# Four transformer layers on one core: in the first layer, another order of the two sequences' energies, the closing norm and the low output sums

## The reference

```
# layer 0, for each token: 16 heads of 16 features
q = x @ Wq;  k = mask * (ctx @ Wk);  v = ctx @ Wv         # 256 -> 256 each
e[x, y] = sum_h q[h, x] * k[h, y]                         # 16 x 16 energies per token
a = softmax_y(e)
o[x, h] = sum_y a[x, y] * v[h, y]
x = layer_norm(x + o @ Wo)                                # * g1 + b1
x = layer_norm(x + relu(x @ W1 + b1) @ W2 + b2)           # * g2 + b2: the closing norm
# layers 1 to 3: each two attentions over 128 tokens and a feed-forward part
```

## Time and profile before

| what | us |
|---|---|
| median of three runs | 2115.61 |
| lowest and highest of them | 2114.29, 2116.65 |
| the profiled execution's own time | 2115.66 |
| its span in the trace | 2113.9 |

### The profile page before, as it was taken

One profiled execution on the slowest core, in us unless ns is written; L12 is line 12 of the kernel. 1 busy time (PEld: TensorE's weight loads), 2 busy tenths in 40 slices (PEclk: granted clock), 3 DMA queues, 4 the chain that ended last, 5 costly groups with the idle time before them and its releaser, 6 DMA issues.

```text
span 2113.9 us, 34721 instructions
## 1 busy us (share of the span) xinstructions
PE 1821.7 (86%) x12417; PEld 1354.7 (64%) x12417; DVE 1280.2 (61%) x2220; ACT 1073.9 (51%) x3134; POOL 996.0 (47%) x1233
## 2 busy tenths in 40 slices
PE   5766666778988998888999999999999999999997
PEld 4655555655665665665666767767667676766766
DVE  5877777856446446446357575674764736546472
ACT  1111111157556557557556555564555656656562
POOL 4566666556346336336425443553544334323340
PEclk8898888877887888887899999999999999999999
DMA  7300000000020000000000200000000000000000
GB/s 192 114 6 5 6 5 5 6 5 1 6 85 1 6 6 1 6 6 1 6 6 7 85 1 6 7 7 6 1 11 1 6 6 2 26 6 1 11 1 11
DMA packets 31361, 35.92 MB, mean 17 GB/s; under 512 B 3196, under 2 KB 30040, under 8 KB 30808
## 3 DMA queue, kind: packets, MB, share of 16 engines
q1 hardware_dynamic: 31192, 33.70, 5.3%
HBM read 31.60 MB, written 2.10 MB: 16 GB/s over the span
## 4 chain that ended last, share of the span: by engine, by line
PE 52%; DVE 13%; ACT 9%; issue 5%; POOL 3%; DVEq 0%; POOLq 0%; ACTq 0%
PE ps L580 27%; PE ps L783 6%; PE ps L722 5%; PE ps L793 5%; PE ps L827 4%; ACT work L957 3%; ACT work L964 2%; DVE work L1151 2%; DVE xn L1011 2%; DVE rowmax L1155 2%; PE ps L593 2%; PE ps L808 1%; POOL work L1344 1%; DVE O L1185 1%; ACT hT L876 1%
## 5 line engine op out<-in xcount | busy, mean ns | idle before, releaser
L580 PE MATMUL ps<-hT,w_slot 128*128 128x256 f32 x1696 | 408.5, 394 | 23.0 <-ACT hT L876 22.0
L1268 POOL TENSOR_TENSOR work<-KT,own_head 128x512 f32<-128x512 f32 x256 | 262.8, 1048 | 285.2 <-PE ps L783 179.8
L580 PEld LDWEIGHTS ps<-hT,w_slot 128*128 128x128 f32 x1696 | 322.4, 196 | 82.6 <-ACT hT L876 27.5
L964 ACT ACTIVATE work<-work,rowmax 128x128 f32<-128x128 f32 x768 | 245.0, 392 | 168.1 <-DVE rowmax L1155 167.4
L793 PEld LDWEIGHTS ps<-ident,work 128*128 128x128 f32 x1536 | 199.3, 153 | 169.8 <-issue 89.8
L957 ACT ACTIVATE work<-ps,rowmax,score_scale 128x128 f32<-128x128 f32 x512 | 229.0, 481 | 119.8 <-DVE rowmax L1159 119.0
L793 PE MATMUL ps<-ident,work 128*128 128x128 f32 x1536 | 265.7, 301 | 17.6 <-ACT work L964 17.2
L783 PE MATMUL ps<-work,QT 128*128 128x512 f32 x512 | 266.4, 605 | 9.7 <-POOL work L1268 4.6
L1344 POOL TENSOR_SCALAR work<-work,winv 128x128 f32<-128x128 f32 x512 | 185.7, 387 | 166.4 <-DVE winv L1171 164.2
L1185 DVE RECIPROCAL O<-ps 128x128 f32<-128x128 f32 x128 | 122.2, 955 | 174.7 <-PE ps L827 174.0
L950 ACT ACTIVATE work<-ps 128x512 f32<-128x512 f32 x256 | 150.8, 596 | 91.0 <-PE ps L793 90.8
(11 more groups left out here) (128 smaller groups left out, 3417.4 us busy)
## 6 DMA issues: line engine op xcount, KB each, us to landing
ctx_in<-in_ctx SPq DMA_DIRECT2D x32, 256.0 KB, 2.7
w_slot<-in_L_xattn_W SPq DMA_DIRECT2D x2, 1024.0 KB, 6.4
w_slot<-in_L_xattn_ff_w SPq DMA_DIRECT2D x1, 2048.0 KB, 11.4
w_slot<-in_L_xattn_ffn_w SPq DMA_DIRECT2D x2, 1024.0 KB, 9.7
w_slot<-in_L_xattn_w SPq DMA_DIRECT2D x2, 1024.0 KB, 8.5
out<-x_all SPq DMA_DIRECT2D x8, 256.0 KB, 2.1
x_all<-in_x SPq DMA_DIRECT2D x1, 1536.0 KB, 11.7
pad<-in_mask_Bx1x1xS_fk SPq DMA_DIRECT2D x1, 1024.0 KB, 9.6
```

What stands on the lines that cost most here:

```text
L580: mm = pe.matmul(dst, lhsT(k), rhs(k), start=(k == 0), stop=(k == chunks - 1))
L964: ex = act.activation(prob[i % NPF][:, tok(h)], src[:, tok(h)], ACT.Exp, bias=shifts[:, at:at + 1])
L1268: pool.tensor_tensor(KB[u % NK].rearrange("p (h k) -> p h k", h=HU), keys, own_head[:, e:HC:2].unsqueeze(2).broadcast_to([P, HU, S]), ALU. ...
```

## The change

Three things are moved; no instruction's form or count changes.

1. The closing `norm`, `scale` and `post` of the ending stream are taken out of the phase and put into the next one, at slots 0, 3 and 7 (`LOCAL_LEFT_SLOT`). There they belong to the stream that is then being mixed. `join` returns them apart, and `joined_pass` hands them on as `left` and `later`. At the end of the first layer they fall into the first two phases of the second.
2. A, of the second sequence, is moved from step 1 to step 4 on VectorE and GpSimd, and its sums on TensorE from step 3 to step 6, behind `tin`. On VectorE the sum, the norms and the closing norm come between the two A.
3. L of the first sequence is moved ahead of B of the second on VectorE. GpSimd's B of the second sequence is moved behind the closing `post`.

```diff
--- before.py
+++ after.py
@@ -142,6 +142,9 @@
 PLAN = [layer_plan(layer) for layer in range(NL)]
 
 
+LOCAL_LEFT_SLOT = {"norm": 0, "scale": 3, "post": 7}
+
+
 def join(layer, after, end, start, tail):
 
 
@@ -157,8 +160,8 @@
     tin = [spot for piece, spot, _, _ in first if piece == "tin"][0]
     pieces = [(at.get(piece, y2 + spot - tin), start, piece, arg, n) for piece, spot, arg, n in first]
     after_y2 = [piece for piece, _, _, _ in last].index("y2") + 2
-    pieces += [(spot, end if i < after_y2 else tail, piece, arg, n) for i, (piece, spot, arg, n) in enumerate(last)]
-    return pieces
+    pieces += [(spot, end, piece, arg, n) for piece, spot, arg, n in last[:after_y2]]
+    return pieces, [(LOCAL_LEFT_SLOT[piece], tail, piece, arg, n) for piece, _, arg, n in last[after_y2:]]
 
 
 SHIFTED = ("norm", "tin", "bias", "post")
@@ -431,13 +434,18 @@
 
                 return ahead(layer, after, st, {"norm": max([slot for slot, _, piece, _, _ in pieces if piece == "keys"], default=9)})
 
-            def joined_pass(layer, g, after):
-
-                for m in range(len(PLAN[layer]) // 2 - 1):
-                    attend(layer, g, 1, m, chain(layer, g, 0, m + 1))
+            def joined_pass(layer, g, after, left):
+
+                last = len(PLAN[layer]) // 2 - 1
+                for m in range(last):
+                    attend(layer, g, 1, m, chain(layer, g, 0, m + 1) + left)
                     attend(layer, g, 0, m + 1, chain(layer, g, 1, m + 1))
-                attend(layer, g, 1, len(PLAN[layer]) // 2 - 1, joined(layer, g, after, 0))
-                attend(*after, 0, 0, joined(layer, g, after, 1))
+                    left = []
+                pieces, later = joined(layer, g, after, 0)
+                attend(layer, g, 1, last, pieces + left)
+                pieces, left = joined(layer, g, after, 1)
+                attend(*after, 0, 0, pieces + later)
+                return left
 
             def ahead_pass(layer, g, after, left):
 
@@ -460,12 +468,12 @@
 
             together(None, 0, chain(0, 0, 0, 0), late)
             attend(0, 0, 0, 0, chain(0, 0, 1, 0))
+            left = []
             for layer in range(FIRST_AHEAD):
                 for g in range(NG - 1):
-                    joined_pass(layer, g, (layer, g + 1))
+                    left = joined_pass(layer, g, (layer, g + 1), left)
                 before_last(layer)
-                joined_pass(layer, NG - 1, (layer + 1, 0))
-            left = []
+                left = joined_pass(layer, NG - 1, (layer + 1, 0), left)
             for layer in range(FIRST_AHEAD, NL):
                 for g in range(NG - 1):
                     left = ahead_pass(layer, g, (layer, g + 1), left)
@@ -540,10 +548,10 @@
         SUM_LAG = 1
         KEYS_AHEAD = 3
         LOCAL_STEPS = {
-            "pe": {2: [0], 3: [1]},
-            "act": {4: [0], 5: [1]},
-            "dve": {0: [("A", 0)], 1: [("A", 1)], 4: [("S", 0)], 5: [("S", 1)], 6: [("W", 0)], 7: [("B", 0)], 8: [("W", 1), ("B", 1)], 9: [("L", 0)], 10: [("L", 1)]},
-            "pool": {0: [("A", 0)], 1: [("A", 1)], 6: [("B", 0)], 8: [("B", 1)]},
+            "pe": {2: [0], 6: [1]},
+            "act": {6: [0], 7: [1]},
+            "dve": {0: [("A", 0)], 4: [("A", 1)], 5: [("S", 0)], 6: [("S", 1)], 7: [("W", 0), ("B", 0)], 8: [("W", 1), ("L", 0)], 9: [("B", 1)], 10: [("L", 1)]},
+            "pool": {0: [("A", 0)], 4: [("A", 1)], 7: [("B", 0)], 10: [("B", 1)]},
         }
         STEPS_OF = {"att": U + ATT_LAG[True] + 1, "local": 11}
         PARTS = 2
```

## The result

The changed kernel takes 2081.52 us (median of 4 runs, 2081.32 to 2082.5), the kernel before 2115.65 (4 runs, 2114.29 to 2116.65): a ratio of 0.984, 95% interval 0.9823 to 0.9857.

What follows compares the result with a forecast made beforehand. No engine is full; a phase is a chain of waits between VectorE, GpSimd and TensorE. −1.9 (phase 1) + 2.7 (phase 2) − 14 (3 to 7) + 0.2 (8) − 5.8 (9, 10) = −18.8 from 2115.66: 2097, range 2084 to 2110.

Steps and rivals of the forecast that it cites:

- three signs of being wrong: Feed-forward starting later than +29.9, GpSimd's last B ending later than +49, or phases 9 and 10 together not shorter.
- the walk: New phase timed step by step, plus times counted from the previous phase's last low sum: 48.3 against 51.1; chance 0.62.
- Second sums 5.5 at the low clock: TensorE's second energy sums, behind `tin` after some 11.5 us idle, run slow: 5.5.
- -2.8 a phase: Phases 3 to 7 of the first layer: 48.3 against 51.1 each, −14 in all.
- Phase 2, +2.7: No closing norm to get rid of, but late rstd and slow sums: last low sum at +45.4, 42.7 before.
- Phase 8, +0.2: Carries 3.2 of tables on VectorE; the walk gives 54.1 against 53.9.
- Phase 1, -1.9: GpSimd's second B starts when VectorE's second product ends, 48.9; last low sum ends at 55.6 for 57.48.
- Layer 2, -5.8: Phases 9 and 10: −3.5 and −3.3 as closing norm and scaling leave Q's path, 1.0 of 6.8 taken as lost.
- the clock stays low: Rival: TensorE's clock rises only half-way through the feed-forward; sums 2.3, products 3.6 longer; 2132 us; chance 0.07.
- The blocks are milder: Rival: L1284 slips in ahead of the product (−1.0), second sums at full clock; 2079 at most; chance 0.11.
- Layer 2 gives it back: Rival: post displaces GpSimd's rounding in the attention, which TensorE's transposes wait for; −13 in all, 2103; chance 0.12.
- No net change: Rival: GpSimd's second A or last B comes 3 later than walked; phases 3 to 7 stay at 51; 2111; chance 0.08.

Runs made afterwards that it cites:

- part 3 alone: Kernel before, with only VectorE's order changed: first low sum ahead of the second B product, without the GpSimd half; 2098.95 us, ratio 0.9903.

## Why the prediction was right or wrong, step by step

Sign and order of events were right, the size was not: 34.1 against 18.8. None of the three signs of being wrong appeared: the feed-forward started ahead of +29.9, GpSimd's last B ended at +44.7, and phases 9 and 10 were shorter. The phase from 142.13 to 189.17, against the walk:

- *A product to +5.2*: 142.04 and 5.11, +5.0. *Second product to +14.2*: +13.8. *rstd +15.2*: +14.7. *Low parts of A to +19.4*: +18.5. *`tin` at +19.8*: +18.8. The walk added whole durations, while in the trace an instruction of VectorE starts 0.1 before its predecessor's recorded end (the earlier trace rows show it: 151.19 and 151.10), and the second scaling was put behind the low parts although it was over with them. So the walk was 1.0 late at `tin`; 1.26 in the mean of the five phases, since phase 3 has it at +17.4.
- *Second sums 5.5 at the low clock*: 5.35, 6.04, 4.77, 5.75 and 6.16, 5.6 in the mean. The feed-forward starts at +24.9 in the mean (23.4 to 25.8), forecast +26.5; what `tin` does not explain of this is the overlap of TensorE's records (167.67 starts ahead of the sums' end, 167.84).
- *From there 21.8 to the end*: 21.5 in all five. The last low sum waits for GpSimd and V is ready within 0.1 of its end (188.46 and 0.60 on ScalarE): the two chains end together, as said.
- Together 1.9 a phase, 10 of the 15 us by which the total missed: **the failed term is "-2.8 a phase", the walk's 48.3, measured -4.8 and 46.35**. Within it, the walk was 1.3 too late at `tin`, another 0.4 from there to the feed-forward and 0.3 behind it. The roundings all went upwards in one long chain, and -2.8 is a difference of two numbers near 50: 4% of the walk was 70% of the gain that it forecast.
- *Phase 2, +2.7*: +0.5. L1292 was held there (3.48), as forecast; again 1.0 is missing ahead of `tin` (+17.7), and the sums took 4.61 and not 5.5.
- *Phase 8, +0.2*: -2.8. The forecast's 54.1 does not follow from its own terms: 48.3 and 3.2 of tables make 51.5, and the phase took 51.2. The tables hold VectorE from 328.87 to 333.21, while GpSimd does its low parts, so the product behind them takes 3.70 and not 5.1. `tin` is at +21.8, the sums take 5.06, and from the feed-forward's start (356.48) to the end it is 23.6.
- *Phase 1, -1.9*: -3.5, of which 1.3 is an earlier start of the first product (15.97 for 17.31). That is not of the change's doing: over the fourteen traces this start varies from 15.97 to 17.31, and the traces of before and after happen to be its two ends.
- *Layer 2, -5.8*: -4.1, the span's 34.0 less the first layer's 29.9. TensorE's V product came +1.7 behind the low sum, as said, and took 1.99 for 3.78. TensorE's timelines tell where the difference went. At the output projection behind phase 10 the changed kernel is 36.3 ahead (460.15 for 496.42), 6.3 of it since the first layer. So phases 9 and 10 gained nearly all of the 6.8 that the prediction counted. This projection then takes 3.67, where before it took 1.99, and at the feed-forward behind it the lead is 34.7 (505.22 for 539.96). The prediction took 1.0 as lost within the two phases; 2.3 were given back behind them, in work whose order is unchanged. The rows, the last one from before:

```profile
381.82 1.99 PE L588 MATMUL ps<-w_slot,hT 128*128 128x256 f32 x8 [1.37 <-DVE QKb L993]
...
460.15 3.67 PE L588 MATMUL ps<-w_slot,OT 128*128 128x256 f32 x8
...
496.42 1.99 PE L580 MATMUL ps<-w_slot,OT 128*128 128x256 f32 x8
```

Of the rivals, *the clock stays low* did not happen: the level was 1.00 from 167.80 on. (Its price was summed too low: 5.9 late in phases 2 to 8 on top of 2097 is some 2138, not 2132.) *The blocks are milder* gives the right time for a wrong reason: its first half failed (3.46 is the full block), and so did its second (5.6 in the mean). *Layer 2 gives it back* is 2.3 of 6.3, a third, and not in the phases that it named. *No net change* was wrong.

On the block, the trace first: L1292, 0.22 alone, took 3.46 beside the product, until 156.02, where the product ended at 155.93, and 0.22 when the product was moved. The Trainium skill (SBUF — State Buffer, "Who interferes with whom") has the shared port pair held for the whole instruction; the trace agrees. What I did not ask is whether the part that brings the block about pays: alone it gains 0.3%, beside the other two it costs 0.6%.

## What to carry to other kernels

Where a gain is a small difference of two long chains, walk the unchanged kernel by the same rules too, and take the difference of the two walks: the roundings then cancel. Price the parts of a combined change one by one; here two of three together were 13 us better than all three, and two edits that gained nothing alone gained 1.9 us a phase together, because they shortened two chains of the same length. To tell which of two chains bounds, look at the last instruction's wait in each variant: here it waited for GpSimd in one and stood behind a wait for TensorE in the other. And see whether TensorE's matmuls run at the low level behind a wait: filling the wait with matmuls that nobody reads gained 2 us a phase in one order and nothing in another, so see first that something waits for what TensorE makes there.

## What the runs showed of the hardware that I had not expected

The same program shows two phase lengths, 48.1 and 51.0, by the point at which the clock returns after 8.3 us of idle time (part 3 alone: 5.24 and 3.98, or 6.72 and 5.47, for the two groups of sums). So a phase length moves by 3 us between phases whose rows up to these sums agree within some hundredths. Whether this also spreads the runs there (2094.14 to 2099.65) was not tested. The Trainium skill (TensorE: Matmul & The Clock Gate, "What's actually happening") says that the moment of the change depends on where the first matmul lands. The trace agrees as far as it goes: the moment differs behind equal idle times, phase by phase of one execution; on what it depends no run here shows.

VectorE's sums of 2048 elements do not meet GpSimd: L1087 took 2.29 and the low parts of A beside it 3.85, as alone. Its scalings of 128x256 do: a single one of L1019 takes 0.41 when GpSimd does nothing and up to 2.01 beside the low parts; the four together took 4.20 or 5.42.
